# A fused four-layer graph network on one core: the second layer's input is split, turned and projected in float16 from inside the first layer's last rounds

## The reference, cut to what matters

```python
# layer 0: attention over neighbours
h = x @ edge_w;  e = where(adj > 0, h @ h.T, -9e15)
x = layernorm(x + adj * (softmax(x @ node_w, axis=0) * softmax(e, axis=1)) @ (x @ weight) + bias)
# layer 1: gated mixture; its entry is what changes
h = x @ W_sa
s_left, s_right = h @ a_sa[0, :256], h @ a_sa[0, 256:]
e = where(adj != 0, exp(-leaky_relu(s_left[:, None] + s_right[None, :], 0.01)), 0)
x_a = e / (e.sum(1) + 1e-5) @ h
gate_a = sigmoid(concat([adj @ x, x]) @ Wa.T + ba)      # gate_b alike
x = layernorm(x + sigmoid(gate_a * x_a + gate_b * (adj @ (x @ W_gcnb) + b_gcnb)))
# layer 2: one normalized graph convolution; layer 3: three graph convolutions, 512 hidden
```

## Time and profile before

| | us |
|---|---|
| runs, median of 3 | 842.82 |
| lowest, highest | 839.61, 854.05 |
| the profiled execution, device time | 841.72 |
| its span, first to last instruction | 839.9 |
| PE busy in the span | 780.1 (93%) |
| DVE, ACT, POOL busy | 445.8, 330.0, 110.6 |
| mean granted TensorE clock | 0.984 |

### The profile page before, as it was taken

One profiled execution on the slowest core, in us unless ns is written; L12 is line 12 of the kernel. 1 busy time (PEld: TensorE's weight loads), 2 busy tenths in 40 slices (PEclk: granted clock), 3 DMA queues, 4 the chain that ended last, 5 costly groups with the idle time before them and its releaser, 6 DMA issues.

```text
span 839.9 us, 11816 instructions
## 1 busy us (share of the span) xinstructions
PE 780.1 (93%) x4223; PEld 517.3 (62%) x4264; DVE 445.8 (53%) x940; ACT 330.0 (39%) x499; POOL 110.6 (13%) x215
## 2 busy tenths in 40 slices
PE   7898999999688999999979999999997999997997
PEld 6766766666476878787845554765663466464343
DVE  4586646667588579797974346211226111012655
ACT  4565546455065446465551123321335222223100
POOL 1011111111370001010111111000002000000343
PEclk9999999999889999999999999999998999999999
DMA  7969999995400000000002000000000000000011
GB/s 197 188 111 188 193 162 184 186 178 101 88 8 13 1 2 1 1 2 1 1 1 82 0 0 1 1 0 0 0 0 26 1 1 0 0 0 0 20 38 44
DMA packets 112571, 42.41 MB, mean 50 GB/s; under 512 B 103312, under 2 KB 109584, under 8 KB 112528
## 3 DMA queue, kind: packets, MB, share of 16 engines
q1 hardware_dynamic: 110224, 33.44, 20.6%
q0 software_dynamic: 2304, 8.39, 6.7%
HBM read 22.95 MB, written 2.10 MB: 30 GB/s over the span
## 4 chain that ended last, share of the span: by engine, by line
PE 53%; issue 24%; DVE 5%; SPq 5%; ACT 5%; DMA 4%; POOL 4%; POOLq 0%; ACTq 0%; DVEq 0%
PE ps L623 10%; PE ps L742 10%; PE ps L720 8%; PE ps L770 6%; PE ps L551 4%; DMA turned<-pl 4%; SPq L343 4%; PE ps L751 3%; PE ps L707 3%; PE ps L563 3%; PE ps L510 2%; POOL x L452 2%; ACT em L808 1%; PE ps L533 1%; PE ps L565 1%
## 5 line engine op out<-in xcount | busy, mean ns | idle before, releaser
L623 PE MATMUL ps<-adjT,x 128*128 128x512 bf16 (+1 forms) x739 | 168.5, 379 | 10.0 <-DVE x L1277 4.6
L623 PEld LDWEIGHTS ps<-adjT,x 128*128 128x128 f16 x768 | 71.7, 98 | 93.0 <-issue 5.7
L563 PE MATMUL ps<-sup,turned 128*128 128x512 f16 x256 | 85.6, 384 | 8.1 <-DMA turned<-pl 7.7
L1022 DVE TENSOR_TENSOR hh_lo<-hf,hh_hi 128x512 fp32r<-128x512 f32 x32 | 22.2, 692 | 117.4 <-ACT hf L968 117.4
L742 PE MATMUL ps<-adjT,G 128*128 x375 | 82.6, 379 | 0.9 <-ACT hf L968 0.4
L648 PE MATMUL ps<-H_hi,es_hi 128*128 128x258 f32 x256 | 76.8, 300 | 4.1 <-DVE es_lo L1022 3.7
L648 PE MATMUL ps<-H_lo,es_hi 128*128 128x258 f32 x256 | 72.4, 283 | 0.0
L648 PE MATMUL ps<-H_hi,es_lo 128*128 128x258 f32 x256 | 72.3, 283 | 0.0
L565 PE MATMUL ps<-sup,turned 128*128 128x256 f16 x256 | 70.4, 275 | 0.0
L742 PEld LDWEIGHTS ps<-adjT,G 128*128 128x128 f16 x384 | 37.3, 98 | 45.4 <-issue 0.9
L770 PE MATMUL ps<-x,adjT 128*128 128x512 f16 x256 | 58.1, 387 | 3.7 <-DVE x L1378 3.7
(11 more groups left out here) (200 smaller groups left out, 1444.2 us busy)
## 6 DMA issues: line engine op xcount, KB each, us to landing
adjb<-in_adj POOLq DMA_DIRECT2D x16, 512.0 KB, 7.2
x<-in_x SPq DMA_DIRECT2D x4, 512.0 KB, 6.2
out<-adjf SPq DMA_DIRECT2D x16, 128.0 KB, 1.7
adjf<-in_L_gnn_W SPq DMA_DIRECT2D x1, 1024.0 KB, 5.8
W1f<-in_L_gnn_W SPq DMA_DIRECT2D x1, 512.0 KB, 3.8
adjf<-in_L_gnn_W SPq DMA_DIRECT2D x1, 512.0 KB, 3.7
we<-in_L_gnn_edge_w SPq DMA_DIRECT2D x1, 256.0 KB, 3.8
w0x<-in_L_gnn_weight SPq DMA_DIRECT2D x1, 256.0 KB, 6.9
```

The costliest lines, as they stand in the source:

```text
L563: ins = mm(bank(6 + u), PT(HI, u)[:, jt, :], sup[:, jt, :], start=(jt == 0), stop=False, skip_group_check=True)
L623: ins = mm(bank(4 + f), x16[:, part, jt, f * P:(f + 1) * P], adj(b, jt), start=(jt == 0 and part == HI), stop=(jt == T - 1 and part == LO))
L1022: return tt(to, frm, high.bitcast(F32), ALU.subtract)
```

## The change

- **SP.** The seven loads of layer 1's weights and the two of its small biases are issued right behind the first loads, ahead of the first adjacency transposes. The bias row is loaded once all 16 `bias_x` are made.
- **Weights.** After round 4 DVE makes the weight products and the largest weight, POOL reduces it over the partitions (in its turn t = 2), and after round 6 DVE makes scaled float16 parts `w16`. The scale is undone in `vj`, `ex` and `rz` by small factors in `gw`.
- **x in float16.** `conv_high` (POOL) runs inside the turns of the last rounds: tiles 0 to 6 behind turn 11, 7 to 11 behind turn 12, then one for each turn. `conv_first` (DVE) makes the low parts between the last `final0` calls. `x16` lies where `adjb` was, so the first waits for all adjacency transposes and masks.
- **Turning and projecting.** PE turns both float16 parts of two tiles in 8 transposes into one bank (`turn16`), ACT copies them out with one instruction of 1024 elements (`turned_read`), and PE projects in float16 (`project16`), six matmuls a tile. `weighted(T - 1)` stands behind the first three turns and four projections. ACT and DVE work on a tile as before, with the `x16` low part made elsewhere.
- **Left scores by turns.** Instead of 24 matmuls, PE transposes column 1 of `ex`, broadcast over 128 columns, 4 transposes for a block; blocks 0 and 1 ahead of layer 1's first block, 2 and 3 in it.
- **Layer 1's first block** does 8 tiles of the neighbour sum ahead of its first pair (`AGG_FIRST`), and DVE splits the gate weights inside it (`gate_parts`).
- **Waits.** The barrier `l0_done` is gone. `normed` of a tile is done at the end of its `final0`'s round, behind `p_low`, and not two rounds later. `bias_x(t)` waits for one `final0` less.

The core of the diff (indentation cut; the removed code of the border is in the listing above):

```diff
 sp.dma_start(brow[:, :], vec_row(b0_in)).then_inc(w0_landed, 16)
+sp.dma_start(wsx[:, :, 0:D], w_tiles(wsa_in)).then_inc(wt1_landed, 16)
+sp.dma_start(arow, asa_in.to_broadcast([P, 2 * D])).then_inc(wt1_landed, 16)
+sp.dma_start(wgx[:, :, 0:D], w_tiles(wg_in)).then_inc(wt1_landed, 16)
+for g, (w, b) in enumerate(((wa_in, ba_in), (wb_in, bb_in))):
+    cols = w.rearrange("a (s k p) -> p s k a", s=2, p=P)
+    sp.dma_start(wgx[:, :, D + g:D + g + 1], cols[:, 0, :, :]).then_inc(wt1_landed, 16)
+    sp.dma_start(wsx[:, :, D + 2 + g:D + 3 + g], cols[:, 1, :, :]).then_inc(wt1_landed, 16)
+    sp.dma_start(bab[:, 0, g:g + 1], vec_row(b)).then_inc(bias1_landed, 16)
...
-sp.wait_ge(sup_lo, TB)
...
-sp.wait_ge(l0_done, 4)
-for g, b in enumerate((ba_in, bb_in)):
-    sp.dma_start(bab[:, 0, g:g + 1], vec_row(b)).then_inc(bias1_landed, 16)
+sp.wait_ge(xb_ready, T)
 sp.dma_start(brow[:, :], vec_row(bg_in)).then_inc(bias1_landed, 16)
...
 def bias_x(t, u, before=0):
-    wait_from(pool, xb_used, before + t)
+    wait_from(pool, xb_used, before + t - 1)
     nc.gpsimd.tensor_tensor(xb[:, u, :], tile(x, t), brow[:, :], ALU.add).then_inc(xb_ready, 1)
...
+def conv_high(t):
+    if t == 0:
+        pool.wait_ge(fill_ready, T)
+        for k in range(AB):
+            pool.wait_ge(adjT_landed[k], 16 * (T // AB))
+    pool.wait_ge(y_normed, t + 1)
+    nc.gpsimd.tensor_scalar(x16[:, HI, t, :], x[:, t, :], XS, None, ALU.mult).then_inc(conv_hi, 1)
+for t in range(T):
     norm_factor(t, t % 2)
-    bias_x(t + 2, t % 2)
+    if t + 2 < T:
+        bias_x(t + 2, t % 2)
     if t + 2 * AB < T:
         load_adj(t + 2 * AB)
...
-pool.wait_ge(l0_done, 4)
+    if t == 2:
+        pool.wait_ge(wsmax_ready, 1)
+        nc.gpsimd.partition_all_reduce(gw[:, 1:2], gw[:, 0:1], P, RMAX).then_inc(wsmax_all, 1)
+    if t == T - 5:
+        for c in range(7):
+            conv_high(c)
+    if t == T - 4:
+        for c in range(7, 12):
+            conv_high(c)
+    if t >= T - 3:
+        conv_high(t - 1)
+conv_high(T - 1)
...
-for t in range(T):
-    nc.gpsimd.tensor_scalar(x16[:, HI, t, :], x[:, t, :], XS, None, ALU.mult).then_inc(conv_hi, 1)
...
+def turn16(g):
+    pe.wait_ge(conv_lo, 2 * g + 2)
+    if g >= 2:
+        pe.wait_ge(t16_read, g - 1)
+    for i in range(2):
+        for part in (HI, LO):
+            for k in range(KD):
+                q = (2 * i + part) * KD + k
+                ins = nc.tensor.transpose(bank16(4 + g % 2)[:, q * P:(q + 1) * P],
+                                          x16[:, part, 2 * g + i, k * P:(k + 1) * P], identb[:, :])
+    ins.then_inc(t16_mm, 1)
+def project16(t):
+    if t == 0:
+        pe.wait_ge(w16_ready, 1)
+        pe.wait_ge(e_read, 2 * T)
+    if t >= 4:
+        pe.wait_ge(p1_hi, t - 3)
+        pe.wait_ge(p1_lo, t - 3)
+    pe.wait_ge(t16_read, t // 2 + 1)
+    for k in range(KD):
+        for p, q in ((HI, HI), (HI, LO), (LO, HI)):
+            ins = mm(bank(t % 4, D + 4), turned16(t, p, k), w16[:, q, k, :],
...
+    ins.then_inc(p1_mm, 1)
...
+def left_row(b):
+    if b == 0:
+        pe.wait_ge(p1_lo, T)
+        pe.wait_ge(pv_read, T)
...
+    for k in range(TB):
+        ins = nc.tensor.transpose(ps[:, 6 + b % 2, k * P:(k + 1) * P],
+                                  ex[:, b * TB + k, 1:2].to_broadcast([P, P]), ident[:, :])
+    ins.then_inc(sl_mm, 1)
 weighted(T - 2)
-weighted(T - 1)
-pe.drain().then_inc(l0_done, 1)
...
+turn16(0)
+for g in range(1, TURNS):
+    if g == 3:
+        weighted(T - 1)
+    turn16(g)
+    project16(2 * g - 2)
+    project16(2 * g - 1)
+project16(T - 2)
+project16(T - 1)
+left_row(0)
+left_row(1)
...
-    first = 0
+    first, tiles = 0, AGG_TILES if b else AGG_FIRST
     wait_from(pe, g_ev, b * TB)
     for pair in range(PAIRS):
-        if pair < len(AGG_TILES):
-            for jt in range(first, first + AGG_TILES[pair]):
+        if pair < len(tiles):
+            for jt in range(first, first + tiles[pair]):
                 for f in range(KD):
                     aggregate_tiles(0, b, f, (jt,))
-            first += AGG_TILES[pair]
+                if b == 0 and jt == 3:
+                    left_row(2)
+                    left_row(3)
+            first += tiles[pair]
+        if b == 0 and pair == 0:
+            pe.wait_ge(H_ready, 2)
         attend(b, pair)
-        if pair == len(AGG_TILES) - 1:
+        if pair == len(tiles) - 1:
+            if b == 0:
+                pe.wait_ge(sl_read, B)
...
-act.drain().then_inc(l0_done, 1)
...
+def turned_read(g):
+    act.wait_ge(t16_mm, g + 1)
+    act.wait_ge(e_read, 2 * T)
+    if g >= KEPT:
+        act.wait_ge(p1_mm, 2 * (g - KEPT) + 2)
+    run(xT16[:, g % KEPT, :], bank16(4 + g % 2), ACT.Copy).then_inc(t16_read, 1)
...
+    own.link(run(vj[:, t, :], ps[:, t % 4, D:D + 1], ACT.Exp, scale=gw[:, 4:5]))
+    run(H[HI][:, t, 0:D], bank(t % 4, D), ACT.Copy, scale=vj[:, t, :]).then_inc(p1_hi, 1)
...
+turned_read(0)
+for g in range(1, TURNS):
+    turned_read(g)
+    projected(2 * g - 2)
+    projected(2 * g - 1)
+projected(T - 2)
+projected(T - 1)
...
+left_row(0)
+left_row(1)
...
-act.wait_ge(p1_lo, P1_SPLITS)
-for pair in range(DEEP):
-    edge_exp(0, pair)
+edge_exp(0, 0)
+left_row(2)
+left_row(3)
+edge_exp(0, 1)
+act.wait_ge(ex_ready, 1)
+run(wi[:, :], ex[:, :, 1], ACT.Exp, scale=SLOPE).then_inc(w_exp, 1)
+edge_exp(0, 2)
...
+def weight_products():
...
+    dve.wait_ge(wt1_landed, 7 * 16)
+    for k in range(KD):
+        for g, c in ((0, D), (1, 0)):
+            own.link(nc.vector.tensor_tensor_reduce(
+                out=scr, in0=wsx[:, k, 0:D], in1=arow[:, c:c + D], scale=1.0, scalar=0.0,
+                op0=ALU.mult, op1=ALU.add, accum_out=wsx[:, k, D + g:D + g + 1]))
+    nc.vector.tensor_reduce(gw[:, 0:1], wsx.rearrange("p a b -> p (a b)"), AX_X, ALU.max,
...
+def weight_parts():
+    dve.wait_ge(wsmax_all, 1)
...
+    own.link(ts(w16[:, HI, :, :], wsx, gw[:, 2:3], None, ALU.mult))
+    stt(w16[:, LO, :, :], wsx, gw[:, 2:3], w16[:, HI, :, :], ALU.mult, ALU.subtract) \
+        .then_inc(w16_ready, 1)
...
+        dve.wait_ge(conv_hi, t + 1)
+        stt(x16[:, LO, t, :], x[:, t, :], XS, x16[:, HI, t, :], ALU.mult, ALU.subtract) \
+            .then_inc(conv_lo, 1)
...
+    own.link(ts(ex[:, t, :], ps[:, t % 4, D:D + 4], gw[:, 3:4], None, ALU.mult))
+    stt(H[LO][:, t, 0:D], bank(t % 4, D), vj[:, t, :], H[HI][:, t, 0:D].bitcast(F32),
+        ALU.mult, ALU.subtract).then_inc(p1_lo, 1)
...
     maxima(t, u)
-    if t >= 5:
-        normed(t - 5, 1 - u, x[:, t - 5, :])
     if t >= 3:
         final0(t - 3, 1 - u)
+    if t == T - 1:
+        conv_first(range(3))
     p_low(t, u)
+    if t >= 3:
+        normed(t - 3, 1 - u, x[:, t - 3, :])
...
     round0(t)
-normed(T - 5, 1, x[:, T - 5, :])
+    if t == 4:
+        weight_products()
+    if t == 6:
+        weight_parts()
+conv_first(range(3, 10))
 final0(T - 3, 1)
...
+conv_first(range(10, 12))
 normed(T - 3, 1, x[:, T - 3, :])
...
+conv_first(range(12, 13))
 for part in (HI, LO):
     own.link(nc.vector.memset(H[part][:, :, D + 1:D + 2].bitcast(F32), 0.0))
+final0(T - 2, 0)
+conv_first(range(13, 14))
+normed(T - 2, 0, x[:, T - 2, :])
+for t in range(4):
+    projected(t)
+final0(T - 1, 1)
+conv_first(range(T - 2, T - 1))
+normed(T - 1, 1, x[:, T - 1, :])
+for t in range(4, 6):
+    projected(t)
+conv_first(range(T - 1, T))
+for t in range(6, T):
+    projected(t)
...
+def gate_parts():
+    split(wgx, wgs)
+    dve.sem_inc(w_ready, 1)
+    dve.wait_ge(bias1_landed, 48)
+    own.link(tt(ex[:, :, 2:4], ex[:, :, 2:4], bab[:, :, :].to_broadcast([P, T, 2]), ALU.add))
+    dve.sem_inc(ex_ready, 1)
+    dve.wait_ge(dinv_ready, 1)
+    ts(dsc[:, :], dinv[:, :], XS, None, ALU.mult).then_inc(dsc_ready, 1)
+    dve.wait_ge(w_exp, 1)
+    own.link(ts(wi[:, :], wi[:, :], EPS, None, ALU.mult))
...
+dve.wait_ge(sl_read, 1)
...
 edge_low(0, 1)
 edge_scores(0, 2)
+gate_parts()
+dve.wait_ge(sl_read, B)
```

More of the change, by code:

```diff
@@ L130, in build @@
         x = sb(ctx, "x", [P, T, D])
+        before = ExitStack()
+        adjb = sb(before, "adjb", [P, AB, N], BF16)
+        before.close()
+        x16 = sb(ctx, "x16", [P, 2, T, D], F16)
         ident = sb(ctx, "ident", [P, P])
-        identb = sb(ctx, "identb", [P, P], BF16)
+        identb = sb(ctx, "identb", [P, P], F16)
         deg = sb(ctx, "deg", [P, T])
@@ L166, in build @@
         lay0 = ExitStack()
+        fill = sb(lay0, "fill", [P, 2, N], BF16)
         hT = pair(lay0, "hT", [P, KD, N])
+        sb(lay0, "rest_of_H", [P, 4 * T])
         sup = sb(lay0, "sup", [P, T, 2 * D], F16)
@@ L182, in build @@
         em = sb(lay0, "em", [P, 2, N])
-        fill = sb(lay0, "fill", [P, 2, N], BF16)
         pre0 = ExitStack()
@@ L198, in build @@
         lay123 = ExitStack()
-        x16 = sb(lay123, "x16", [P, 2, T, D], F16)
+        pre1 = ExitStack()
+        xT16 = sb(pre1, "xT16", [P, KEPT, GROUP], F16)
+        pre1.close()
         agg = pair(lay123, "agg", [P, KD, CB])
@@ L204, in build @@
         slrow = sb(lay1, "slrow", [P, N])
```

(52 more changed lines are left out.)

98 lines of the change are left out of this document (26 added, 72 removed).

## The result

| | before | changed |
|---|---|---|
| runs in one comparison, median, us | 847.92 (20 runs) | 831.97 (20 runs, 825.78 to 847.07) |
| ratio to before, interval | | 0.984 (0.981 to 0.987) |
| the profiled execution, device time | 841.72 | 831.39 |
| its span | 839.9 | 829.6 |
| granted clock | 0.984 | 0.986 |

The ratio leaves out the runs that fell into the chip's slower state, so it isn't the quotient of the two medians. The change is worth 1.6%. A second comparison, on another chip, gave 835.84 us against 842.8 and a ratio of 0.990 (0.984 to 0.995). The forecast was 825, a ratio of 0.979. In the two profiled executions the device time falls by 10.3 us where the working had 17.4 less 0.8.

What follows compares the result with a forecast made beforehand. PE, busy for 93% of the span, was taken to bound the kernel: attend(0, 0) 13.9 us earlier plus 3.5 of neighbour sum gives 17.4, 841.7 to 824.3; 0.8 for the clock makes 825, range 818 to 834.

Steps and rivals of the forecast that it cites:

- Nothing of the front changes until `maxima(15)` ends at 205.40: All rounds up to the end of maxima(15) on DVE were taken as unmoved, ending at 205.40 us.
- POOL's reduction falls into a round on an engine that is busy for 13% of the span.: In the rounds, POOL's reduction of the largest weight was taken to cost nothing.
- The sign is open ... I take nothing: In the rounds, earlier adjacency loads could lose or win up to 3.5 us; nothing was counted.
- the rivals (828.5, chance 0.1): Rounds: earlier adjacency loads get ahead of awaited turned tiles and hold the rounds up; 828.5 us, chance 0.1.
- Uncovered it would be 4.7: DVE's weight products and parts in rounds 5 and 7: free within DVE's waits, 4.7 us if not covered.
- The stretch: From maxima(15) ending at 205.40 to the first attend(0, 0), forecast at 250.3 instead of 264.24 us.
- the clock term of 0.8: Before the left rows: PE idles 2 us and a lowered clock costs 0.8, half of an earlier 1.7 us.
- The rival of POOL and DVE shutting each other out: Last rounds and tail: conversions take longer than 0.94 us; at 2.5 each the time is 846 us; chance 0.03.
- The next two tiles: Tail: DVE waits for POOL's factor and conversion, 1.7 us for tile 14, then 0.85 and 0.94 again.
- The rival of half the clock: Tail: PE's clock falls near 229.5 to 232 and stays, turning and projecting at half speed; 831 us, chance 0.15.
- rivals with transposes at 0.20 us each: Turning on PE: float16 transposes no cheaper than float32 ones, 1.6 us a turn16; 828 us, chance 0.05.
- the signs named for a wrong forecast: Slow conversions, late p_low(15), changed turned-tile waits in rounds, clock under 0.8 from 232 to 245, PE awaiting es_lo.

Runs made afterwards that it cites:

- e11: The kernel before with only bias_x waiting for one final0 less, so adjacency loads start up to a round earlier; ratio 1.0032 (1.0001 to 1.0063).
- e1: The changed kernel with weight products and POOL's reduction moved to the start; 833.18 us, ratio 0.9875.
- e5: The changed kernel with weight products and reduction at the start and adjacency loads waiting again for the later final0; 826.31 us, ratio 0.9815.
- e14: The kernel before, unchanged, for a second trace; 843.61 us.
- e15: The kernel before, unchanged, for a third trace; 849.67 us.
- e9: The changed kernel again, unedited, in a second comparison on another chip; 835.84 us, ratio 0.990.
- e12: The changed kernel with only POOL's tail order edited: conversion 13 right behind 12, conversion 14 ahead of the last factor; 829.65 us, ratio 0.983.
- e13: Repeat of e5: the changed kernel with reduction at the start and later adjacency loads; 829.11 us, ratio 0.980.
- e7: e5 with ACT instead of POOL making the high parts of tiles 0 to 11; 826.29 us, ratio 0.9815.
- e6: e5 with POOL's tail order edited: conversion 13 right behind 12, conversion 14 ahead of the last factor; 825.57 us, ratio 0.979.
- e8: The changed kernel with four cures: reduction at start, later adjacency loads, POOL's tail order, ACT making high parts 0 to 11; 824.68 us, ratio 0.979.
- e10: Repeat of e8, the changed kernel with all four cures, beside the changed kernel on the same chip; 825.13 us, ratio 0.976.
- e2: The changed kernel with only the weight products moved to the start, the reduction left in turn 2; 839.52 us, ratio 0.989.

## Why the prediction was right or wrong

**"Nothing of the front changes until `maxima(15)` ends at 205.40"** is the step that failed. Of the 8 us between the two `attend(0, 0)` points (250.3 forecast, 258.36 measured), 5.4 are there. Three steps of the working and one of the reading made it up:

- *"POOL's reduction falls into a round on an engine that is busy for 13% of the span."* It was costed at nothing by a busy share. It is 0.38 us of work and 14.2 us of POOL standing still, in a turn in which the next factor was asked for 7.4 us after the last load. The same pauses stood in the trace of before, each with a `MODIFY_POOL_CONFIG` (at 40.3, 63.2 and 636.6): 8.4 us ahead of the three reductions of the start, 10.3 ahead of POOL's first `bias_x` behind them, and the 7.50 shown above. I read the rows of the start as the start's own business. The right bound would have been the nearest row with a reduction in it, with what stands around it. The Trainium skill (GPSIMD Engine Reference, Instruction dispatch) says that the first call of a freshly loaded kernel on this engine pays about 6 us with no instruction to show for it. From the `MODIFY_POOL_CONFIG` to the reduction it is 5.7 to 6.1 us in four of six traces, which agrees (8.7 and 8.8 in two); from the one on the way back to the next `tensor_tensor` it is 6.9 to 7.7, a pause of the same kind and somewhat longer. The reduction was not new at that point, it had run at 47 to 50 us, so the price was paid anew at the change, and in both directions. It was the rule that spoke against this change, and I had not weighed it.
- *"The sign is open ... I take nothing"*, for the adjacency loads that start earlier. The mechanism and the size were in the rivals (828.5, chance 0.1), the sign was not open: e11 measured 2.7 us of loss (0.1 to 5.3) for that edit alone, and with the reduction at the start e1 (earlier loads) is at 0.9875 where e5 (later loads) is at 0.9815. 6.7% of DMA for the loads was the wrong row to weigh it by. The DMA share from 60 us to the rounds' end was 1.07 in the trace of before and is 0.99 in the changed kernel: a load that starts earlier there has hardly any free time to go to.
- *"Uncovered it would be 4.7"*, for DVE's weight work. `weight_products` cost nothing that shows. `weight_parts` was covered in e5 (PE's waits for maxima are the 1.0 us of before), but in the changed kernel it stood behind the late factor, and its 1.95 us lie in PE's wait of 3.09.
- *The baseline.* The trace of before ended its rounds 3.5 us ahead of the mean of three (208.8), and its granted clock from 60 us to the rounds' end was 1.00 where e14 and e15 have 0.98: a part of the forecast rested on a lucky trace. The device time hid that, being only 1.1 us under the median of runs. The changed rounds' own traces (changed, e9, e12) have a mean of 214.9, so the loss is 6 us rather than 5.4; by the medians of runs, where e5, e13 and e7 stand against the changed kernel and e9, it is 2 to 8.

**The stretch: right in its mechanism, 2.7 us longer than the 44.9 forecast,** of which the clock term of 0.8 had covered a part. Measured between the same two points it is 47.6 (by the rounds' end 46.5 to 48.8 in seven traces with this tail). Counted from its start:

- *The factor of tile 13* is 1.6 us late (13.2 behind the start, forecast 11.6). `p_low(15)` began 3.5 us behind it, as forecast, but took 2.89 instead of 2.36 beside `bias_x(14)`; the conversions took 1.10 and 1.22 us on the mean (7.67 for 7, 6.08 for 5) instead of 0.94, and DVE's low parts waited for them. The rival of POOL and DVE shutting each other out was there, at its small end. On this the Trainium skill (SBUF — State Buffer, SBUF: two separate sides) has the shared pair of ports held for a whole instruction by one or the other. In the changed kernel `bias_x(14)` takes 1.75 us where it takes 0.72 alone, and e7 has the delay of `p_low` with the conversions gone: both agree. The conversions agree too, one by one, which their means hide: the first of each group starts beside a `p_low` instruction and takes 1.72 and 1.71 us, one behind it 1.24, those beside the low parts of `x16` 0.99 to 1.13, and the others 0.85. They weren't kept out for all of `p_low`, as the forecast read it: the page speaks of one instruction, and `p_low` is two.
- *The next two tiles* held DVE for 1.9 us each (factor, then conversion), where the forecast had 1.7 and 1.8, and with them it falls another 0.6 behind. They were rightly counted as a cost. What the forecast missed is that the cost needn't be there: e6 takes 3.7 us off the stretch with the order of three instructions.
- *The last tiles* took 0.9 us more: PE ran at 0.83 of the clock from 240 to 250, after idling 1.96 and 2.20 us, though ACT's tile was cheaper than taken (0.66 against 0.72). That is the clock term, forecast at 0.8. The rival of half the clock did not come.
- *Left rows and first sums* took 8.6 us for 9.0.

**What held.** `turn16` (0.5 forecast for 8 transposes; 0.61 measured at full clock, 1.06 for 16), `turned_read` (1.0; 0.97 to 1.02), the projection (0.7 a tile; 1.49 for two at full clock), the wait ahead of the last `weighted` gone, PE's pause of "about 2.5 us near 230 and 2 near 240" (1.96 at 232, 2.20 at 239.7, DVE behind both by its times, though the trace names no releaser), full clock from 214 to 229 (but 0.87 in the rounds, behind the reduction), the nine early loads and DVE's `weight_products` free, `attend` in the first block with its parts in time (PE 41.3 of 41.6 us busy from 258.4 to 300), and the rest of the span shorter by 4.2 us on the means (575.2 of five traces, 571.0 of twelve) for the 3.5 taken. The rivals with transposes at 0.20 us each and with a slower kernel fell. Of the signs named for a wrong forecast three came: conversions over 1.1 us, `p_low(15)` later than 209, and, in e9 though not in the profiled execution, 13.0 us of waits for turned tiles.

**The best kernel.** The change with the four cures (e8, e10): 824.7 and 825.1 us, 0.979 and 0.976 of before. That it is the forecast's number is in part luck: what the forecast had costed at nothing is taken out (e5 and e13, with that alone, have 0.9815 and 0.980), and POOL's order in the tail gives 3.7 us that the forecast had counted as a cost.

**Open.** How the clock, the DMA queue and POOL's hold combine in one round isn't settled: a late turned tile came 40 us behind the reduction in e2, and in e9 DVE never waited for POOL's factor and the rounds still ended at 216.5, behind 13.0 us of waits for turned tiles. Nor is why a DMA transpose takes 2.9 us in one round of e15 and 11.4 in the next. An adjacency load was issued just ahead of it (96.23) and another beside it (106.94), but such loads stand in the rounds around it too.
